# Second expert layer of a two-layer decoder: token lists of 256 rows, two lists a step, and its weights split during the attention layer and kept in DRAM

## What is computed

```python
o_inter = jnp.einsum('bhmd,bhde->bhme', qi * q_decay, kv)
qk = jnp.einsum('bhmd,bhnd->bhmn', qi, ki) * diag_decay
o_intra = jnp.einsum('bhmn,bhne->bhme', qk, vi)
```

```python
scores = jax.nn.sigmoid(logits) + gate_b
weights, indices = jax.lax.top_k(scores, TOP_K)
weights = weights / weights.sum(-1, keepdims=True)
shared_out = jax.nn.silu(x @ w1_shared) * (x @ w3_shared) @ w2_shared
h1 = jnp.einsum('btd,edc->btec', x, w1_routed)
h2 = jnp.einsum('btd,edc->btec', x, w3_routed)
h3 = jax.nn.silu(h1 * h2)
experts_out = jnp.einsum('btec,ecd->bted', h3, w2_routed)
routed_out = jnp.einsum('bted,bte->btd', experts_out, router_probs)
```

## Time and profile before

| | |
|---|---|
| median of 3 executions | 2535.58 us (2535.2 to 2537.73) |
| the profiled execution | 2540.95 us |
| its span | 2539.1 us |
| TensorE busy | 1734.3 us, 68% |
| VectorE busy | 1682.9 us, 66% |
| ScalarE busy | 1294.5 us, 51% |
| POOL busy | 1166.5 us, 46% |
| lightning attention | from about 728 to 1256 us of the span |
| second expert layer | 2128.4 to the end |

### The profile page before, as it was taken

One profiled execution on the slowest core, in us unless ns is written; L12 is line 12 of the kernel. 1 busy time (PEld: TensorE's weight loads), 2 busy tenths in 40 slices (PEclk: granted clock), 3 DMA queues, 4 the chain that ended last, 5 costly groups with the idle time before them and its releaser, 6 DMA issues. The chain is left out here.

```text
span 2539.1 us, 43354 instructions
## 1 busy us (share of the span) xinstructions
PE 1734.3 (68%) x15388; PEld 1103.5 (43%) x15388; DVE 1682.9 (66%) x2876; ACT 1294.5 (51%) x1759; POOL 1166.5 (46%) x1056
## 2 busy tenths in 40 slices
PE   6875677347689999999856366666666653169972
PEld 3332455235367777777645122222222222146641
DVE  5997545632655555555565799999999964923345
ACT  4654454312254444444333388888888862624430
POOL 0000243243403333333223488888888862853326
PEclk8996787679889999999877555555555556579985
DMA  3000210358321211111000155656556644568824
GB/s 100 0 0 0 72 37 25 70 112 171 96 43 42 42 41 41 41 41 31 1 25 0 28 106 108 107 106 109 107 107 107 109 77 82 146 137 161 153 86 130
DMA packets 490251, 190.45 MB, mean 75 GB/s; under 512 B 416045, under 2 KB 482421, under 8 KB 490101
## 3 DMA queue, kind: packets, MB, share of 16 engines
q1 hardware_dynamic: 479349, 159.06, 30.7%
q0 software_dynamic: 10752, 29.37, 5.1%
HBM read 66.70 MB, written 23.07 MB: 35 GB/s over the span
## 5 line engine op out<-in xcount | busy, mean ns | idle before, releaser
L2003 POOL CAST xnT<-xl 128x2048 bf16<-128x2048 uint8 x256 | 483.5, 1889 | 15.8 <-DMA xl<-xh 0.5
L2038 PE MATMUL psum<-e_KT,e_QT 48*128 48x512 bf16 x1024 | 265.0, 618 | 272.0 <-DVE ctxT L2071 124.8
L2071 DVE TENSOR_SCALAR_CACHE_REDUCE ctxT<-psum,e_nsq 128x1024 f32<-128x1024 f32 x256 | 314.7, 1282 | 11.5 <-PE psum L2038 10.1
L2071 DVE TENSOR_SCALAR_CACHE_REDUCE e_Smore<-psum,e_nsq 128x1024 f32<-128x1024 f32 x256 | 314.7, 1282 | 1.7 <-issue 0.4
L2089 ACT ACTIVATE xh<-e_Smore,e_ebias 128x2048 uint8<-128x2048 f32 x128 | 256.2, 2002 | 48.7 <-POOL e_ebias L2010 48.7
L2089 ACT ACTIVATE xh<-ctxT,e_ebias 128x2048 uint8<-128x2048 f32 x128 | 256.3, 2002 | 47.2 <-POOL e_ebias L2010 47.2
L1551 POOL TENSOR_TENSOR d_sq<-d_oS 128x512 f32<-128x512 f32 x60 | 92.3, 1538 | 332.6 <-ACT d_oS L1601 332.6
L118 PE MATMUL psum<-xh,d_T 128*128 128x512 f16 x768 | 219.8, 382 | 3.4 <-ACTq L1559 3.2
L2038 PEld LDWEIGHTS psum<-e_KT,e_QT 48*128 48x128 bf16 x1024 | 34.1, 107 | 401.8 <-DVE ctxT L2071 190.0
L574 POOL TENSOR_TENSOR c_Wx<-c_Wgu,c_Wx 128x512 f32 (+1 forms) x18 | 26.1, 1447 | 383.7 <-ACT c_WdH L568 383.7
L2048 PEld LDWEIGHTS psum<-e_Vi,xnT 128*128 128x128 bf16 x4096 | 119.3, 104 | 112.5 <-issue 104.2
(11 more groups left out here) (404 smaller groups left out, 4342.6 us busy)
## 6 DMA issues: line engine op xcount, KB each, us to landing
kept_y<-ctxT SPq DMA_DIRECT2D x20, 512.0 KB, 3.7
kept_y<-c_y SPq DMA_DIRECT2D x12, 512.0 KB, 5.4
d_Wn<-in_L_attn_w_qkv SPq DMA_DIRECT2D x16, 384.0 KB, 3.5
f_Z<-in_L_ffn_w_routed SPq DMA_DIRECT2D x32, 176.0 KB, 2.5
kept_rows<-xnT SPq DMA_DIRECT2D x8, 512.0 KB, 3.6
xl<-xh SPq DMA_TRANSPOSE x256, 3.1
ctx_rows<-in_ctx SPq DMA_DIRECT2D x1, 2048.0 KB, 8.8
X<-in_x SPq DMA_DIRECT2D x1, 2048.0 KB, 14.2
```

Of the source, the lines that this page charges most:

```text
L2003: pool.tensor_copy(PT[:, sl, :], P8[:, sl, :, :].rearrange("p c q -> p (c q)").bitcast(U8)).then_inc(unpacked, 1)
L2038: mm = pe.matmul(m.bank[pair_banks(c + odd) + q], QT[rows, n // 2, :], KTt[rows, n % H // 2, col:col + BLK], start=True, stop=True)
L2071: dve.tensor_scalar(S32[sl][:, hf * HALF:(hf + 1) * HALF].rearrange("p (a b) -> p a b", a=2), m.psum[:, b:b + 2, :], nsq[:, n + odd:n + od ...
```

## The change

Three parts. First, `KeptWeights`: the weights of the second expert layer are loaded, scaled and split during lightning attention, one expert per head for heads 0 to 13 (in the step of block 2), the other three in the last two heads, and written to DRAM as one block of 128 x 2560 fp16 words per expert; the expert layer then loads 17 such blocks of 640 KB with one DMA each. Second, lists are padded to 256 rows, and a step takes two groups of 256 rows instead of four of 128, so that the first product's matmuls have 256 columns. Third, the room is now 4 x 2048 + 16 x 256 = 12288 slots, 96 tiles, 24 routed steps. The last matmul of `down` reads 128 partitions instead of 48, which the clearing of the padding allows.

```diff
-F_SLOTS = 80 * P
+F_WIDE = 2 * P
+F_SLOTS = 4 * TOK + 16 * F_WIDE
+F_WORDS = 2560
...
+class KeptWeights:
...
+    def clear(self, pool):
+        pool.memset(self.WS[:, :], 0.0).then_inc(self.cleared, 1)
+        pool.memset(self.W2[:, :, :], 0.0).then_inc(self.cleared, 1)
...
+    def scalar(self, act, n):
+
+        act.wait_ge(self.w_in, 80 * n + 80)
+        act.activation(self.W13[:, :, :, :], self.W13[:, :, :, :], ACT.Copy, scale=SPLIT)
+        act.activation(self.W2[:, :, :], self.W2[:, :, :], ACT.Copy, scale=SPLIT).then_inc(self.scaled, 1)
+        act.wait_ge(self.scaled, n + 1)
+        act.wait_ge(self.kept, 16 * n + 16)
+        for hi, src in self.parts(0):
+            last = act.activation(hi, src, ACT.Copy)
+        last.then_inc(self.high, 1)
+
+    def gpsimd(self, pool, n):
+
+        pool.wait_ge(self.high, n + 1)
+        for (lo, src), (hi, _) in zip(self.parts(1), self.parts(0)):
+            last = pool.tensor_tensor(lo, src, hi, ALU.subtract)
+        last.then_inc(self.split, 1)
+
+    def keep(self, sp, n):
+
+        sp.wait_ge(self.split, n + 1)
+        sp.dma_start(self.kept_w[n * P:(n + 1) * P, :], self.WS[:, :]).then_inc(self.kept, 16)
...
+        EVENLY, LATELY = 2, [(0, 1), (0, 3), (1, 1)]
...
                     turn(sp, h)
                     if h + 1 < NH:
                         weights(sp, h + 1)
+                    KW.keep(sp, h - 1)
+                    KW.load(sp, h)
...
+                    for q in range(SPH):
+                        square(h, q)
+                        if q == EVENLY:
+                            KW.gpsimd(pool, h)
...
                             root(slice(0, NT - TPB))
+                        if last and (u, q) in LATELY:
+                            KW.scalar(act, NH - 2 + LATELY.index((u, q)))
+                        elif not last and q == EVENLY:
+                            KW.scalar(act, h)
                         act.wait_ge(squared, 2 * s + 2)
                         act.wait_ge(mixed, s + 1)
                         act.activation(oS[:, q % 2, :], m.bank[5][:, :], ACT.Copy).then_inc(ocopied, 1)
...
+    GPQ = BLK // F_WIDE
...
-        R = Dispatch(m, "f", own, norm, TOP, TILES, 1.0 / (HS * SPLIT), P,
+        R = Dispatch(m, "f", own, norm, TOP, TILES, 1.0 / (HS * SPLIT), F_WIDE,
...
+                    sp.dma_start(W[:, e, :], KW.kept_w[e * P:(e + 1) * P, :]).then_inc(w_in, 16)
...
-                for e in range(NE + 1):
-                    W13, W2 = staged(e % STAGES)
-                    pool.wait_ge(high, e + 1)
-                    for (lo, src), (hi, _) in zip(parts(e, 1, W13), parts(e, 0, W13)):
-                        pool.tensor_tensor(lo, src, hi, ALU.subtract)
-                    pool.tensor_tensor(W2L[:, e], W2, W2H[:, e], ALU.subtract).then_inc(split, 1)
...
-                split_high(0)
-                split_high(1)
                 R.scalar_scores(act, m.bank[6])
-                for e in range(2, NE + 1):
-                    split_high(e)
...
-                    hidden(s, [of(e) for e in es], lambda j, x, k: XG[:, s % TURNED, j, x * KC + k, :])
+                    hidden(s, [up_weights(e) for e in es],
+                           lambda j, x, k: XG[:, s % TURNED, j * TPB // GPQ:(j + 1) * TPB // GPQ, x * KC + k, :])
...
-                                 (hh[:, sl, 1, tok], H1), (hh[0:FB, sl, 1, tok], L1))
+                                 (hh[:, sl, 1, tok], H1), (hh[:, sl, 1, tok], L1))
...
-                pe.wait_ge(split, NE + 1)
+                pe.wait_ge(w_in, 16 * (NE + 1))
```

More of the change, by code:

```diff
@@ L2144, in _, with experts_top4 @@
                             mm.then_inc(outp, 1)
-def experts_top4(nc, m, w, rows_dram, y_dram, out):
+def experts_top4(nc, m, w, KW, rows_dram, y_dram, out):
     NE, F, FB, TOP = 16, 176, 48, 4
-    UPPER = slice(64, 64 + FB)
+    UPPER = KW.UPPER
     HS = 256.0
@@ L2156, in experts_top4 @@
     STEPS = QUADS + NBLK
-    STAGES, STAGED = 4, KC * 2 * F + 2 * D
+    GPQ = BLK // F_WIDE
     GOT, TURNED, GSLOTS = 2, 3, 16
     AT_ONCE = 13
-    (gate_in, loaded, cleared, scaled, high, split, up, copied, product, hmade, hhigh, hready, downs, evac_act, evac_dve, summed,
+    (gate_in, loaded, cleared, w_in, up, copied, product, hmade, hhigh, hready, downs, evac_act, evac_dve, summed,
      combined, stored) = (m.sem(f"f_{n}") for n in (
-        "gate_in", "loaded", "cleared", "scaled", "high", "split", "up", "copied", "product", "h", "hh", "hready", "downs", "evac_act",
+        "gate_in", "loaded", "cleared", "w", "up", "copied", "product", "h", "hh", "hready", "downs", "evac_act",
         "evac_dve", "summed", "combined", "stored"))
-    w_in = [m.sem(f"f_w{i}") for i in range(STAGES)]
     fetched = [m.sem(f"f_fetched{i}") for i in range(GOT)]
@@ L2229, in _ @@
                     load(R.wa[:, 1, :], w["L1_ffn_gate_w"][:, P:2 * P].rearrange("e p -> p e"), gate_in)
-                weights(0)
+                sp.wait_ge(KW.kept, 16 * (NE + 2))
                 load(gb[:, :], w["L1_ffn_gate_b"].partition_broadcast(P))
                 R.constants(load, w)
-                weights(1)
+                for e in range(2):
+                    weights(e)
                 for b in range(NBLK):
@@ L2461, in routed_down @@
                         pe.wait_ge(evac_dve, s - 1)
-                    def of(j):
-                        at = lambda x, rows, part: x[rows, ds(es[j], 1), part, :].rearrange("p o d -> p (o d)")
-                        every = slice(0, P)
-                        return at(W2H, every, 0), at(W2H, every, 1), at(W2L, every, 0), at(W2L, slice(0, FB), 1)
-                    down(s, of)
+                    down(s, lambda j: down_weights(es[j * GPQ // TPB]))
                 def shared_down(s):
@@ L2475, in shared_down @@
                         pe.wait_ge(evac_dve, s - 1)
-                    down(s, lambda j: (W2H[:, NE, 0, :], W2H[:, NE, 1, :], W2L[:, NE, 0, :], W2L[0:FB, NE, 1, :]))
+                    down(s, lambda j: down_weights(NE))
                 def experts(qd):
-                    word = pe.value_load(R.expert[0:1, qd:qd + 1], min_val=0, max_val=NE ** TPB - 1)
-                    return [pe.snap((word >> (4 * j)) & (NE - 1)) for j in range(TPB)]
+                    word = pe.value_load(R.expert[0:1, qd:qd + 1], min_val=0, max_val=NE ** GPQ - 1)
+                    return [pe.snap((word >> (4 * j)) & (NE - 1)) for j in range(GPQ)]
                 R.tensor_logits(pe, m.bank[6])
@@ L2549, in build @@
             experts_top2(nc, m, w, W, kept_rows, kept_y)
-        lightning_attention(nc, m, w)
+        kept_w = nc.dram_tensor("kept_w", (17 * P, F_WORDS), F16, kind="Internal").ap()
+        with ExitStack() as first:
+            KW = KeptWeights(m, w, first, kept_w)
+            lightning_attention(nc, m, w, KW)
         quantised_attention(nc, m, w)
-        experts_top4(nc, m, w, kept_rows, kept_y2, out)
+        experts_top4(nc, m, w, KW, kept_rows, kept_y2, out)
 def kernel(**inputs):
```

115 lines of the change are left out of this document (62 added, 53 removed).

## The result

| | before | the change |
|---|---|---|
| median, same chip | 2535.39 us (4 runs) | 2517.07 us (2515.59 to 2518.48, 4 runs) |
| ratio | | 0.9935, 95% interval 0.9919 to 0.9952 |
| the profiled execution, its span | 2540.95, 2539.1 us | 2515.59, 2513.8 us |
| predicted | | 2533 us, range 2507 to 2563 |

A second comparison of the same two kernels on another chip gave 0.9953 (0.9934 to 0.9971), so the gain is 12 to 18 us. The measured 2517 us lies inside the forecast's range, and "faster by over 0.2%" was the likeliest of its three outcomes (0.46). But the forecast itself said no change that counts, at 2533 us. It was 16 us too high, and one term, the loss in lightning attention, accounts for that.

A forecast was written before the change was run, and what follows sets the result against it. TensorE was taken to bound lightning attention, DMA the changed routed steps. Span 2539.1 + 31 (lightning attention) - 32 (expert layer) = 2538, median 2534.6, given as 2533 us, range 2507 to 2563.

The forecast's parts named there:

- Lightning attention, 17 x 1.8 = 31 us: Lightning attention: each of 17 splits delays the chain to yl, so TensorE waits 1.8 us each, a 31 us loss.
- The forecast as summed: Whole kernel: the terms added up to 2533 us, own range 2518 to 2549, chance 0.50.
- rival 2: Lightning attention: output matmuls have 1.3 us more room, so the stall is 0.5 us; 2510 us, chance 0.13.
- POOL against VectorE, costed at nothing: Lightning attention: POOL's three subtractions a split could stretch VectorE's work by 1.4 us a head, 24 us; costed at nothing.
- rival 4: Last routed steps, second expert layer: empty steps cost nothing extra, 4 x 3.4 us less; 2519 us, chance 0.06.
- rival 3: Routed steps: TensorE stays the bound at 6.8 us a step, 19 x 0.6 = 11 us less; 2522 us, chance 0.12.
- Start of the expert layer: Second expert layer: list 41 us after the scores, not 61.4; first matmul 13.6 after first gather; weight blocks cost 0.
- A routed step: Second expert layer: TensorE needs 6.8 us, not 9.85, but DMA binds at 7.4 a step; bounds 6.7 and 9.85.
- Rival 1: Routed loop's gather, transpose and keep: DMA slows further, 9.0 us a step, +30 us; 2563 us, chance 0.14.
- Empty steps: End of the routed steps: four steps gathering only token 0, slow gathers, 10.8 us each.
- The tail: From the last routed up to the gathers back: 18 us plus 4 for a lowered clock, 22 us.
- Rival 5: Routed steps: TensorE's waits bring 1.2 GHz, 12.8 us a step, +50 us over half of them; 2583 us, chance 0.05.

The follow-up runs named there:

- e2_half: The change with POOL squaring only 256 of 512 columns of oS in the steps that carry a split: 2527.84 us, ratio 0.9977 to the kernel before.
- e8_before_nosum: The kernel before with POOL's sum of squares in lightning attention cut from 512 columns to 8: 2529.21 us, ratio 0.9996 to the kernel before.
- e1_early: The change with the split's five ScalarE operations ahead of the gate's copy, not behind it: 2503.13 us, ratio 0.9869 to the kernel before.
- e6_got3: The change with three gather buffers in place of two in the second expert layer: 2497.59 us, ratio 0.9855 to the kernel before.
- e7_all: The change with the split ahead of the gate's copy, empty slots spread over other rows and three gather buffers: 2473.66 us, ratio 0.9767 to before.
- e5_spread: The change with empty list slots naming rows of their own in place of token 0: 2508.24 us, ratio 0.9889 to the kernel before.

## Where the prediction failed and where it held, point by point

**Lightning attention, 17 x 1.8 = 31 us: the failed step.** Each part of the chain up to yl's start was late nearly as forecast (yl by 1.95 us for 2.1). The step that failed is "Less the margin of 0.34 TensorE waits 1.9 us for yl": it kept yl's 1.70 us as if that were its own work. 0.95 us of it was a wait for POOL's sum; delaying the chain by 1.95 us moved yl from 0.12 us behind the sum's start to 0.07 us ahead of it. The term is 17 x 0.78 = 13.2 us. That was shown from both sides, by e2_half (8.7 us more when POOL is first again) and e8_before_nosum (0.75 us when the sum is cut). With 13 in place of 31 the prediction's own sum gives a span of 2520 us and a median of 2515 to 2517; 2517.07 was measured.

**The range.** The forecast as summed had 2518 to 2549 us of its own and was missed by 1 us. The stated 2507 to 2563 held the result only because rival 2 stretched it, and rival 2's reason was not the one at work: that the range held is in part luck.

**POOL against VectorE, costed at nothing.** The prediction weighed this contention for what the new subtractions would do to the mask and the sums, found it free, and was right: e1_early loses nothing by them. It did not ask the same of the operation on the critical chain, yl, which reads two SBUF tiles beside a POOL operation in nearly every step. The rule of the Trainium skill that it named (GPSIMD Engine Reference) was the right one, put to the wrong instructions: e2_half and e8_before_nosum agree with it.

**Rival 2, the burst is hidden**, with a stall of 0.5 us, was nearest in the place that failed (0.78), but for a reason it did not give: there was no more room than the one step showed, the chain itself got shorter. By the time alone rival 4 (2519) and rival 3 (2522) come nearer than its 2510, and both fell.

**Start of the expert layer.** Scores to first gather 41.6 us for a forecast of 42.2 (41.4 to the list, measured 40.7); first gather to first product 12.8 for 13.5; the 11 MB of weight blocks cost nothing.

**A routed step.** 7.58 us for 7.4 (7.5 to 7.8 in all profiles with two buffers), and TensorE waited for transposes as said, 10.1 us in six of the steps from 2240 to 2366: the first layer was the right model. A step in which TensorE waited for no transpose took 6.5 (2260.20 to 2266.66) for 6.8. Rival 1 (9.0) and rival 3 (6.8) fell; e6_got3 (7.15) and e7_all (7.03) show that rival 3 was little more than one buffer away.

**Empty steps.** 10.75 for 10.8, and rival 4 (nothing extra) fell. That they agree to 0.05 us is luck: the three other profiles of the same routed code have 8.9 to 10.3. Spreading the rows took 11 to 13 us off the stretch (e5_spread), more than the 8 us that the wide lists gained in it with the empty steps.

**The tail** took 18.4 us for 22: I had added 4 us for a lowered clock, and it was granted 0.80 from 2372 to 2404, but 0.98 from there to 2428. **Rival 5**, the slow clock, fell: 0.98 in the routed steps (2260 to 2360 us).

**From span to median.** The profiled execution of before lay 5.6 us above its median and that of the change 1.5 below, so the spans differ by 25.3 us and the medians by 18.3; that difference between two profiles, like the 4.8 us to the scores, was not to be foreseen. The span came out 6.5 us below the 2520.3 that the sum gives with the right term, and the distance from span to median moved the other way: that 2515 to 2517 and 2517.07 lie so close is partly luck too.

## What to carry to other kernels

A duration on a critical chain can hold a wait of its own. Where VectorE and POOL both work on SBUF, look at which of the two started first: the same operation took 0.75 or 1.70 us for 0.2 us of difference in start, so moving a chain changes the lengths in it, in either direction. Put a burst where its engine stands idle for at least the burst's length: here 2.90 us ahead of the gate's copy, against 0.36 one operation later, for a burst of 2.8. And padded work is not free for gathers: give its slots different rows. Where a step's gathers wait for the transpose of two steps before, try a third buffer.

## What the runs showed of the hardware that was not expected

- Of two operations on POOL and VectorE that both read SBUF the earlier one ran at its own length and the later one did most of its work after it: yl, 0.75 us alone, ended 0.55 us after the sum in the steps shown and in the 59 steps of the kernel before where the sum was ahead, and the sum, 1.27 us alone, took 1.81 when yl was ahead. Cutting POOL's first operation by half made the kernel 6 to 11 us slower.
- Gathers that read one and the same row 128 times filled the queues (share 1.04) at 139 GB/s, with one transpose and one keep beside them; gathers of different rows, with transposes and keeps beside them, ran at 234 GB/s at a share of 0.98 (e7_all).
- VectorE's row table of 2048 elements took 2.28 us in the change (2.28 or 2.29 in all four) and 3.24 beside POOL's splits before (all four). The timeline of the kernel before:

```profile
2187.26 3.24 DVE L1091 TENSOR_TENSOR ctxT<-f_iota,f_row 128x2048 f16<-128x2048 f32 x1
```

And of the change, the same operation:

```profile
2186.59 2.28 DVE L1093 TENSOR_TENSOR ctxT<-f_iota,f_row 128x2048 f16<-128x2048 f32 x1
```
